# A graph network's gather ring: GpSimd waits for TensorE's count of products by a constant, instead of for slots that SyncE hands back from a table

## The reference, cut to what matters

```
agg  = segment_sum(h[src], dst)                        # layer 0 (SAGE-like)
out  = segment_sum(support[edge_col] * edge_val, row)  # layer 1, done as a scatter
out  = segment_sum(h[src] * norm, dst)                 # layer 2, three times
msg  = relu(x[src] + edge_attr); agg = segment_sum(msg, dst)   # layer 3
```

## Time and profile before

| | |
|---|---|
| median of 3 runs, no profiler | 7366.6 us |
| span of the profiled execution | 8074.1 us |
| busy GpSimd / TensorE matmul / VectorE / ScalarE | 5199.4 / 4409.3 / 2662.5 / 866.9 us |
| stretch of each gather stage, first gather to last product | 1221 us in stage 0, 1153 in stage 2, 1148 in 3 and 4, 1172 in 5 |
| instructions | 63990 |

### The profile page before, as it was taken

The page is one execution under the profiler, slowest core; times in us unless marked ns, Lnnn a source line. Parts: engine busy times, 40 slices in busy tenths (PEclk is TensorE's granted clock), DMA queues, the critical chain, the costliest instruction groups (busy, mean ns, idle before and its releaser), DMA issues.

```text
span 8074.1 us, 63990 instructions
## 1 busy us (share of the span) xinstructions
PE 4409.3 (55%) x16498; PEld 3303.5 (41%) x16498; DVE 2662.5 (33%) x5948; ACT 866.9 (11%) x2041; POOL 5199.4 (64%) x4804
## 2 busy tenths in 40 slices
PE   3455559866666651444445444445544545556557
PEld 2344338755444440333334333334333334334336
DVE  5443212655555544111112111112111114544445
ACT  0000002322322220000002000002000001000002
POOL 4776660188888883666663666663666663677774
PEclk9777779988888875777777677667777667766768
DMA  2333334166666665333332333333333333666662
GB/s 64 95 104 103 97 90 136 19 72 71 72 72 72 71 72 177 89 91 94 91 94 86 87 93 93 92 93 94 88 93 93 92 91 101 185 182 185 184 182 64
DMA packets 497711, 811.01 MB, mean 100 GB/s; under 512 B 97410, under 2 KB 367636, under 8 KB 497364
## 3 DMA queue, kind: packets, MB, share of 16 engines
q0 software_dynamic: 300288, 615.29, 34.2%
q1 hardware_dynamic: 197076, 191.58, 7.4%
HBM read 652.63 MB, written 153.86 MB: 100 GB/s over the span
## 4 chain that ended last, share of the span: by engine, by line
another core or an unknown queue 28%; PE 25%; POOL 20%; issue 17%; DVE 6%; DMA 2%; DVEq 1%; SPq 0%; ACT 0%; POOLq 0%; ACTq 0%
PE acc L608 17%; POOL sums_by_src L488 11%; POOL ring L466 9%; DVE onehot L1123 3%; PE acc L532 3%; PE acc L527 2%; PE high L527 1%; DVEq L1122 1%; DVE X L1154 1%; PE high L518 1%; DMA ring<-table_x,idx_dst 1%; DMA sums_by_src<-ring,E 1%; PE high L532 1%; PE acc L518 0%
## 5 line engine op out<-in xcount | busy, mean ns | idle before, releaser
L608 PE MATMUL acc<-ring,onehot 128*128 x8320 | 2738.6, 490 | 2828.7 <-DVE onehot L1123 1780.1
L608 PEld LDWEIGHTS acc<-ring,onehot 128*128 128x128 f32 x8320 | 1958.4, 246 | 3581.4 <-issue 3237.5
L466 POOL DMA_INDIRECT ring<-table_g,idx_dst x2346 | 2290.3, 976 | 1338.0 <-issue 683.5
L1123 DVE TENSOR_TENSOR onehot<-iota_row,dl_dst 128x512 f32<-128x512 f32 x1040 | 720.3, 694 | 3556.4 <-remote 2262.8
L488 POOL DMA_INDIRECT sums_by_src<-ring,E x782 | 1208.1, 1545 | 613.0 <-ACT high L925 373.9
L466 POOL DMA_INDIRECT ring<-table_x,idx_dst x782 | 833.1, 1065 | 418.8 <-issue 343.1
L466 POOL DMA_INDIRECT ring<-in_x_dram,idx_dst x782 | 792.2, 1013 | 407.8 <-issue 243.3
L768 PE MATMUL high<-H,ring 128*128 x1664 | 546.1, 485 | 455.3 <-ACT high L925 441.6
L768 PEld LDWEIGHTS high<-H,ring 128*128 128x128 f32 x1664 | 375.3, 236 | 550.7 <-issue 490.0
L870 ACT COPY H<-acc 128x256 f32<-128x256 f32 x196 | 72.9, 372 | 4461.8 <-PE acc L608 2781.7
L1365 DVE TENSOR_SCALAR ring<-acc,E 128x128 f32<-128x128 f32 x832 | 283.7, 402 | 575.9 <-PE acc L536 575.9
(11 more groups left out here) (259 smaller groups left out, 2914.9 us busy)
## 6 DMA issues: line engine op xcount, KB each, us to landing
E<-in_edge_attr_dram SPq DMA_DIRECT2D x781, 128.0 KB
ring<-table_g,idx_dst POOLq DMA_INDIRECT x2346
table_g<-H SPq DMA_DIRECT2D x147, 128.0 KB, 1.7
ring<-sums_by_src SPq DMA_DIRECT2D x36, 512.0 KB, 4.8
sums_by_src<-ring SPq DMA_DIRECT2D x2, 6272.0 KB, 38.8
ring<-in_x_dram,idx_dst POOLq DMA_INDIRECT x782
sums_by_src<-ring,E POOLq DMA_INDIRECT x782, 3.8
ring<-table_x,idx_dst POOLq DMA_INDIRECT x782
```

What stands on the lines that cost most here:

```text
L466: pool.indirect_dma_start(out=ring_v[:, b % SLOTS, 0:D], out_offset=None, in_=table[name][:, :], in_offset=bass.IndirectOffsetOnAxis(ap=id ...
L608: pe.matmul(acc4[:, ds(to, width)], onehot[:, (q * BATCH + j) % ONEHOTS, :], ring[:, ds(slot, width)], start=False, stop=True, skip_group_ ...
L1123: last = tt(onehot[:, s:s + BATCH, :], iota_row[:, :].unsqueeze(1).to_broadcast((P, BATCH, P)), dl_ap[which][:, q * BATCH:(q + 1) * BATCH] ...
```

## The change

`free_slots` and the constant BEHIND are gone, with them SyncE's wait for `tables_done`; the relay now waits for a landing and counts `landed` up, and nothing else (beside the loads of x). In every gather stage GpSimd waits ahead of group k >= 16 until `summed` of this stage is at least 4(k + 1) - 64 + 49.

```diff
--- before.py
+++ after.py
@@ -18,7 +18,6 @@
 GROUPS = SLOTS // BATCH
 ONEHOTS = 8
 EAS = 8
-BEHIND = 4
 ZG = 13
 Y0 = 40
 YS = 2
@@ -243,20 +242,10 @@
             def weights(k, name):
                 load(wt[k][:, :, :], a[name].rearrange("(h k) n -> k h n", k=P), sm("weights_in"))
 
-            def free_slots(n, k):
-
-                if 0 <= k < GB - GROUPS:
-                    last_pair = sp.value_load(need[AGGS[n][0]][0:1, k:k + 1], min_val=1, max_val=PAIRS + 1)
-                    sp.wait_ge(sm(f"summed{n}"), last_pair)
-                    sp.sem_inc(sm("freed"), 1)
-
             def relay(n):
                 for k in range(GB):
                     sp.wait_ge(*landing(n, k))
                     sp.sem_inc(sm(f"landed{n}"), min(BATCH, B - k * BATCH))
-                    if k == BEHIND and n == 0:
-                        sp.wait_ge(sm("tables_done"), n + 1)
-                    free_slots(n, k - BEHIND)
                     t = y_step(k, -10) if n == 0 else None
                     if t is not None:
                         if t >= YB:
@@ -450,10 +439,7 @@
                     pool.wait_ge(sm(f"summed{n - 1}"), PAIRS + 1)
                 for k in range(GB):
                     if k >= GROUPS:
-                        if n < 5:
-                            pool.wait_ge(sm("freed"), before_stage(n) * (GB - GROUPS) + k - GROUPS + 1)
-                        else:
-                            pool.wait_ge(sm(f"summed{n}"), (k + 1) * BATCH - SLOTS + T)
+                        pool.wait_ge(sm(f"summed{n}"), (k + 1) * BATCH - SLOTS + T)
                     here = range(k * BATCH, min(B, (k + 1) * BATCH))
                     if features:
                         if k >= 2:
```

## The result

The changed kernel takes 7399.1 us, median of 4 runs (7389.7 to 7401.5), against 7367.1 us for the kernel before. The ratio is 1.0039, 95% interval 1.0027 to 1.0052: 32 us, slower.

What follows compares the result with a forecast made beforehand. GpSimd's issue was taken as the pace of all gather stages. SyncE's part 0, stages 2 to 4 0 and stage 0 30 us on 7366.6 gave 7397 us, range 7340 to 7470.

Steps and rivals of the forecast that it cites:

- The choice on which all rested: All gather stages: GpSimd's issue sets the pace at 1.25 us a block, 978 us a stage; the profile's stalls are the profiler's.
- My account of the surplus: Profiled execution of the kernel before: GpSimd's waits (512 us) and stage ends (150 us) explain 662 of 707.5 us.
- Stage 0: 30 us: GpSimd's first reuse waits for thirteen quads, 39.6 us later; 24 blocks made up at 1.25 us cost 30, between 0 and 39.6.
- The lower end of my range for this term: Stage 0: 20 us if the thirteen quads run a third faster beside a silent GpSimd; range 7385 to 7410.
- Stages 2 to 4: 0 us: GpSimd arrives 8 us after the product it needs, slack growing 1.25 us a tile; cost 0, bound 65 us.
- SyncE's part: 0 us: Removing SyncE's 4 x 180 table loads, waits and increments costs 0; bounds 0 and a gain of 44 us.
- my bound of 44 us: Largest gain from SyncE's part: VectorE's 71 us of waits for the relay less 3 x 9 us of landings.
- The sign that I named for the profile: Changed kernel's stage 0: GpSimd's first wait near 106 us instead of 66.6, ended by TensorE, 13 quads ahead of it.
- Waits for TensorE early in stages 2 to 4: Expected sign in the changed kernel's profile: GpSimd waits ended by TensorE's L608, early in these stages; no size given.
- The delay is not swallowed: Answers the rival that TensorE paces later stage 0, so GpSimd's early delay costs nothing: 7367 us, chance 0.23.
- The ring does not leak: Answers the rival that TensorE pauses over 8 us near stage starts outlast 15 slots: 95 us, 7462 us, chance 0.12.
- SyncE was not in the way: Answers the rival that the relay passed landings on late, so freeing it gains up to 44 us: 7323 us, chance 0.10.

Runs made afterwards that it cites:

- the second profile: The kernel before, run and profiled once more unchanged: 7360.9 us, ratio 0.9996.
- the dose: Changed kernel, stage 0's first reuse waiting for 7 or 28 products instead of 52: 7371.1 us (ratio 1.0001) and 7381.9 us (1.0017).
- the near-exact wait without SyncE: Changed kernel, stage 0's constant allowing 4 tile borders plus one per 14 blocks instead of all 49: 7371.1 us, ratio 1.0001.
- 10 us taken: Changed kernel, GpSimd's wait in stages 2 to 4 asking for 8 products (two quads) more: 7394.5 us, ratio 1.0040 against the kernel before.
- 15 us taken: Changed kernel, GpSimd's wait in stages 2 to 4 asking for 12 products more: 7441.9 us, ratio 1.0105 against the kernel before.

## Why the prediction was right

It gave 7397 us, with the sum 0 + 0 + 30 us; measured were 32 us (and 28 us for the changed kernel on another chip, 29 us for the constant in stage 0 alone). Point by point:

- *The choice on which all rested* (GpSimd's issue is the pace of the timed kernel, the stalls of the profile are not in it) holds: the second profile of the kernel before has no stall, and first to last gather take 981 us in stage 2, for which 978 had been reckoned. My account of the surplus, 662 of 707.5 us by GpSimd's waits and the ends of the stages, left out that the making of the tables was stretched as well: the first quad starts at 128.45 us in the second profile and at 164.09 us in the earlier trace rows. So not all of the first wait of 66.6 us was real, as I had it; 30.2 us are.
- *Stage 0: 30 us.* Predicted as 39.6 us of later restart less the contention that GpSimd escapes, 9.6 us. Measured: 42.0 us, less 12.5 us; both are 2 to 3 us larger than reckoned, and it is luck that these two errors cancel. Mechanism and size are both confirmed, the one by the runs with the constant in single stages, the other by the dose: 33, 50 and 72 us of waiting. The lower end of my range for this term, 20 us if the thirteen quads ran a third faster beside a silent GpSimd, had no ground: from the first to the thirteenth quad's start it is 39.9 us with GpSimd at work (128.45 to 168.38 in the second profile) and with GpSimd silent (131.60 to 171.52). The contention slows GpSimd and not VectorE.
- *Stages 2 to 4: 0 us.* Right. The slack at the first reuse, 8 us by my reckoning, is 9 to 10 us by both runs that took from it (10 us taken: a wait of 0.5 to 1.1 us; 15 us taken: one of 4.7 to 6.3 us, the sequencer's 0.3 taken off), and behind it it grows faster than I said.
- *SyncE's part: 0 us.* Right: the near-exact wait without SyncE takes what the kernel before takes. The 71.0 us in 36 times from which my bound of 44 us came were the disturbed execution's; in the second profile VectorE waits 724 times for the relay, 2958.7 us, and the time does not fall when SyncE has less to do, so these waits are for landings.
- *The sign that I named for the profile* was wrong in its number: I expected a first wait near 106 us and it is 72.2 us. The 66.6 us from which I started held some 36 us of that execution's stretching. The difference between the two waits was right. Waits for TensorE early in stages 2 to 4, which I had also named, don't show: none there is over 0.3 us. Thirteen quads do stand ahead of the first wait's end.
- *The rivals.* The delay is not swallowed: there is no later wait in stage 0 to swallow it. The ring does not leak: stage 5's 21.7 us at its seventeenth group were the disturbed execution too; in the changed kernel's profile stage 5 has no wait for TensorE over 0.3 us. SyncE was not in the way. The rule of the Trainium skill on consistent gaps (Perfetto Trace Analysis, Optimization Strategy) fits the first profile, whose ring was full again and again; in the undisturbed profiles of both kernels GpSimd stands before a full ring once, at its first reuse in stage 0.

No version here beats the kernel before. The constant in stages 2 to 4 with the table in stage 0 equals it, with less work on SyncE.

## What to carry to other kernels

Ahead of any reading, set the profiled span against the times without the profiler; where it is 10% longer, decide first which waits the timed runs can hold, for here every wait for a slot after the first was the profile's own. A bound for the worst case costs nothing where producer and consumer run in step and the slack covers its looseness (here some 9 us to spare; 15 us more of looseness cost 16 us a stage), and costs the time of all the work that it waits for in excess at the one place where the consumer starts late with the buffer full. What a paused engine escapes (here a neighbour's contention, 12.5 of 42 us) must be taken off the price of its pause.

## What I had not expected of the hardware

One execution with the profiler ran 715 us (9.7%) longer than another of the same instructions, with stalls of some 18 us between quads and a releaser that the profile could not name. The other eleven profiles, of this kernel, the changed one and their variants, have spans within 4 us of their times. With GpSimd's gathers at 950 ns and 300 ns between them, the 782 of stage 2, 3 or 4 came out at 980 to 984 us in ten of these eleven, whether the wait ahead of a group was for SyncE's count or TensorE's; the eleventh, with three quads more, took 996 to 999 us. And a VectorE tensor_tensor operation lengthened a gather (0.95 us to as much as 1.80) only where it was under way at the gather's start; one that started within the gather did not.
